# Router logits computed transposed and turned back: weights and moving operand swapped in one product of a fused transformer kernel

## The reference

```python
h = tok_ref(x, ...)                      # 16 images, 196 patches x 768 -> 192, plus class token
h = concatenate([h, txt], axis=1)        # 16 x 325 rows of 192
h = h + attn_ref(layernorm(h), ...)      # q, k, v; scores * decay mask; no softmax
y = layernorm(h)
# the expert layer, all 5200 rows:
logits = y.astype(float32) @ Wg.T        # 128 experts
sig = sigmoid(logits)
choice = sig + e_bias
topk_idx = top_k(choice, 6)              # 6 experts of 128 for every row
topk_w = take(sig, topk_idx); topk_w = 2.5 * topk_w / sum(topk_w)
# every expert takes its first 192 rows: silu(x Wg) * (x Wu) @ Wd, weighted, added back
# plus a shared expert on all rows
h = h + routed + shared
```

## Time and profile before

| | |
|---|---|
| runs | 699.82, 701.12 and 701.9 us, median 701.12 us |
| the profiled execution | 699.24 us, span 697.4 us |
| PE busy | 678.6 us (97%) |
| PEld, DVE, ACT, POOL busy | 635.5, 469.4, 332.0, 201.4 us |
| mean granted TensorE clock | 0.990 of full speed |
| chain that ended last | PE 80%, DVE 10%, issue 4%, ACT 2% |

### The profile page before, as it was taken

The page is one execution under the profiler, slowest core; times in us unless marked ns, Lnnn a source line. Parts: engine busy times, 40 slices in busy tenths (PEclk is TensorE's granted clock), DMA queues, the critical chain, the costliest instruction groups (busy, mean ns, idle before and its releaser), DMA issues.

```text
span 697.4 us, 16667 instructions
## 1 busy us (share of the span) xinstructions
PE 678.6 (97%) x4613; PEld 635.5 (91%) x4614; DVE 469.4 (67%) x1490; ACT 332.0 (48%) x803; POOL 201.4 (29%) x309
## 2 busy tenths in 40 slices
PE   6989999999999999999999999999999999999997
PEld 6879988899988888799999999999999999999997
DVE  2357878888788878765666566666675757576653
ACT  2245555565555666444445343434444434343543
POOL 3022223223223210202323233333333242424240
PEclk9899999999999999999999999999999999999999
DMA  7236434545344321733445454545454545454542
GB/s 232 89 99 210 129 112 148 158 154 152 115 137 141 108 95 63 182 61 63 95 103 108 104 103 106 105 106 104 105 107 102 106 102 107 98 108 97 103 88 56
DMA packets 75188, 79.54 MB, mean 114 GB/s; under 512 B 6505, under 2 KB 67065, under 8 KB 75162
## 3 DMA queue, kind: packets, MB, share of 16 engines
q1 hardware_dynamic: 62538, 65.69, 33.9%
q0 software_dynamic: 11760, 12.31, 11.6%
q10 hardware_dynamic: 864, 1.25, 0.6%
HBM read 51.91 MB, written 19.32 MB: 102 GB/s over the span
## 4 chain that ended last, share of the span: by engine, by line
PE 80%; DVE 10%; issue 4%; ACT 2%; DVEq 1%; POOL 1%; POOLq 0%; ACTq 0%
PE bank L1275 24%; PE bank L1243 12%; PE bank L1292 8%; PE bank L1073 8%; PE bank L1255 8%; PE bank L1061 6%; PE bank L1293 4%; PE bank L1103 3%; PE bank L1217 2%; DVE stats L1454 1%; DVE w_raw L1565 1%; PE bank L1131 1%; PE bank L1088 1%; DVE y_B L1474 1%; DVE h L1490 1%
## 5 line engine op out<-in xcount | busy, mean ns | idle before, releaser
L1740 DVE TENSOR_TENSOR s_inter<-s_gate,bank 128x384 f32<-128x384 f32 (+1 forms) x112 | 60.2, 539 | 73.2 <-PE bank L1275 67.0
L906 ACT ACTIVATE s_gate<-bank 128x384 f32<-128x384 f32 (+1 forms) x112 | 53.5, 478 | 79.1 <-PE bank L1275 79.0
L1292 PE MATMUL bank<-s_dn,s_in_hi 128*128 128x384 f32 (+1 forms) x287 | 88.9, 371 | 0.3 <-DVE s_in_lo L1748 0.2
L727 POOL DMA_INDIRECT result<-y_rows,put_idx x40 | 59.8, 1496 | 57.8 <-DVE y_rows L1727 42.1
L1275 PE MATMUL bank<-all_hiA,s_hi 128*128 (+4 forms) x210 | 73.9, 352 | 0.6 <-DVE s_inter L1740 0.6
L1293 PE MATMUL bank<-s_dn,s_in_lo 128*128 128x192 f32 (+1 forms) x287 | 72.9, 254 | 0.0
L1073 PE MATMUL bank<-w_tok,patches 128*128 128x192 f32 x360 | 68.4, 343 | 4.2 <-DMA patches<-xp 4.0
L798 ACT ACTIVATE y<-h,shift,rstd 128x192 f32<-128x192 f32 (+2 forms) x96 | 45.6, 538 | 54.9 <-POOL shift L658 54.9
L1275 PE MATMUL bank<-all_B,s_lo 128*128 (+4 forms) x210 | 70.2, 334 | 0.0
L1275 PE MATMUL bank<-all_B,s_hi 128*128 (+4 forms) x210 | 70.2, 334 | 0.0
L1275 PE MATMUL bank<-all_loA,s_hi 128*128 (+4 forms) x210 | 70.0, 333 | 0.0
(11 more groups left out here) (216 smaller groups left out, 1831.5 us busy)
## 6 DMA issues: line engine op xcount, KB each, us to landing
raw_gu<-wgu SPq DMA_DIRECT2D x22, 464.0 KB, 5.4
raw_gu<-wgu SPq DMA_DIRECT2D x44, 232.0 KB, 6.0
patches<-xp SPq DMA_DIRECT2D x15, 588.0 KB, 4.3
down_w<-wdn SPq DMA_DIRECT2D x22, 348.0 KB
result<-s_rows POOLq DMA_DIRECT2D x12, 288.0 KB
result<-h SPq DMA_DIRECT2D x16, 192.0 KB
yw_rows<-y SPq DMA_DIRECT2D x16, 192.0 KB
all_hiA<-y_hiA SPq DMA_DIRECT2D x16, 162.5 KB, 2.6
```

The lines of the kernel that those rows point to most:

```text
L727: pool.indirect_dma_start(acc[:, :], bass.IndirectOffsetOnAxis(ap=put_idx[:, h:h + 1], axis=0), y_rows[:, h, :], None, compute_op=ALU.add) ...
L906: act.activation(s_gate[m % 2][0:r, 0:width], up_banks(m, alone)[0][0:r, 0:width], ACT.Silu).then_inc(s_gate_ready, 1)
L1292: pe.matmul(bank[0:r, 0:2 * D], s_in_hi[:, m, rows], s_dn[:, m, :], start=m == 0, stop=False)
L1740: dve.tensor_tensor(s_inter[m % 2][0:r, 0:width], s_gate[m % 2][0:r, 0:width], up, ALU.mult).then_inc(s_inter_ready, 1)
```

## The change

`logits(n)` swaps the two sides: the router matrix is the weights (128 columns) and all S + 1 = 326 columns of the transposed rows move, so five passes do the whole block and the result stands transposed, expert by partition. ACT copies it to SBUF (`lg_evac`, tile `lgT`), in the place where `sigmoid(n)` stood. PE turns it back with three transposes (`turn_logits`) in the next step, behind `turn(n1, n+1)` and ahead of `tokens`, into the same bank. `sigmoid(n)` then runs in ACT's next step, between `turned` and `normed(n2)`. In the tail both are placed by hand between parts of the shared expert.

```diff
--- before.py
+++ after.py
@@ -224,6 +224,7 @@
         cum = sb("cum", [128, 3, SP], BF16)
         patches_1 = sb("patches_1", [128, KC, 256])
         addend_1 = sb("addend_1", [128, D])
+        lgT = sb("lgT", [E, SP])
         zero = left[0:CH, :, :].rearrange("p t n -> p (t n)")[:, 0:YW]
         raw_tables = h1[0:1, :, :].rearrange("p t n -> p (t n)")[:, 0:TABLES]
 
@@ -345,6 +346,8 @@
         pv_mm = sem("pv_mm")
         h1_ready = sem("h1_ready")
         lg_mm = sem("lg_mm")
+        lgT_ready = sem("lgT_ready")
+        lg_turned = sem("lg_turned")
         sig_ready = sem("sig_ready")
         choice_ready = sem("choice_ready")
         best_ready = sem("best_ready")
@@ -806,8 +809,13 @@
                     act.activation(q_B[:, :], qB_ps[0:DB + 1, 0:S], ACT.Identity,
                                    bias=b_q[0:DB + 1, 1:2]).then_inc(qk_ready, 1)
 
+                def lg_evac(n):
+                    act.wait_ge(lg_mm, n + 1)
+                    wait(act, lg_turned, n)
+                    act.activation(lgT[:, 0:S], lg_ps[:, 0:S], ACT.Copy).then_inc(lgT_ready, 1)
+
                 def sigmoid(n):
-                    act.wait_ge(lg_mm, n + 1)
+                    act.wait_ge(lg_turned, n + 1)
                     wait(act, wraw_ready, 3 * n)
                     act.activation(sig[:, 0:2, :], lg_ps[:, 0:2 * E].rearrange("p (t e) -> p t e", t=2), ACT.Sigmoid)
                     act.activation(sig[0:TL[2], 2, :], lg_ps[0:TL[2], 2 * E:3 * E], ACT.Sigmoid).then_inc(sig_ready, 1)
@@ -836,6 +844,7 @@
                     if more:
                         turned(n + 1)
                     if not isinstance(n, int) or n > 0:
+                        sigmoid(n - 1)
                         normed(n2, h1, n)
                     if more:
                         q_evac(n + 1)
@@ -850,7 +859,7 @@
                         normed(n1, h0[:, by_turns(n + 2), :], n + 2)
                     if not isinstance(n, int) or n > 0:
                         weights(n - 1)
-                    sigmoid(n)
+                    lg_evac(n)
 
                 def shared_hi(half, i):
                     act.wait_ge(s_in, 48 + 96 * half)
@@ -940,15 +949,17 @@
                 _, width, tiles = AHEAD[0]
                 last = B - 1
                 turned(last)
+                sigmoid(last - 2)
                 normed(n2, h1, last - 1)
                 q_evac(last)
                 counts(last - 2)
                 split_hi(last - 1)
                 weights(last - 2)
-                sigmoid(last - 1)
+                lg_evac(last - 1)
                 act.wait_ge(h0_ready, B)
                 act.wait_ge(tok_mm, B)
                 s_silu(0, width, 0, PACKED)
+                sigmoid(last - 1)
                 s_silu(0, width, 1, PACKED)
                 normed(n2, h1, last)
                 s_hi_part(0, width, 0)
@@ -960,9 +971,10 @@
                 s_hi_part(0, width, 2)
                 s_silu(0, width, 4, PACKED)
                 act.activation(table_of[:, :], half_neg[0:1, 0:1], ACT.Sigmoid)
-                sigmoid(last)
+                lg_evac(last)
                 s_hi_part(0, width, 3)
                 s_silu(0, width, 5, PACKED)
+                sigmoid(last)
                 s_hi_part(0, width, 4)
                 s_silu(0, width, 6, PACKED)
                 s_hi_part(0, width, 5)
@@ -1133,12 +1145,18 @@
 
                 def logits(n):
                     pe.wait_ge(n2["s_lo"], n + 1)
+                    passes = ((n2["hiA"], g_hi[:, 0, :]), (n2["hiA"], g_lo[:, 0, :]), (n2["loA"], g_hi[:, 0, :]),
+                              (n2["st"], g_hi[:, 1, :]), (n2["st"], g_lo[:, 1, :]))
+                    for i, (x, w) in enumerate(passes):
+                        mm = pe.matmul(lg_ps[:, 0:SP], w, x[:, :], start=i == 0, stop=i == 4)
+                    mm.then_inc(lg_mm, 1)
+
+                def turn_logits(n):
+                    pe.wait_ge(lgT_ready, n + 1)
                     for t in range(3):
                         r, o = TL[t], t * 128
-                        data = (n2["hiA"][:, o:o + r], n2["loA"][:, o:o + r], n2["st"][:, o:o + r])
-                        mm = split_product(lg_ps[0:r, t * E:(t + 1) * E], data, [g_hi[:, h, :] for h in range(2)],
-                                           [g_lo[:, h, :] for h in range(2)])
-                    mm.then_inc(lg_mm, 1)
+                        mm = pe.transpose(lg_ps[0:r, t * E:(t + 1) * E], lgT[:, o:o + r], ident[:, :])
+                    mm.then_inc(lg_turned, 1)
 
                 def running_counts(n):
 
@@ -1154,6 +1172,8 @@
                     if more:
                         turn(n1, n + 1)
                     begun = isinstance(n, int) and n == 0
+                    if not begun:
+                        turn_logits(n - 1)
                     if ahead:
                         tokens(n + 2, 1 if begun else 0)
                     if more:
@@ -1323,6 +1343,7 @@
                 at, width, tiles = AHEAD[0]
                 data = moving(at, width)
                 turn(n1, last)
+                turn_logits(last - 2)
                 pe.wait_ge(h0_ready, B)
                 pe.wait_ge(s_lo_set, 2 * PIECES)
                 pe.wait_ge(big_out, 48 * 4)
@@ -1338,12 +1359,15 @@
                     if m == 3:
                         pe.wait_ge(h1_ready, B)
                     s_up(0, data, width, m, PACKED, PACKED_FREE[m])
+                    if m == 1:
+                        turn_logits(last - 1)
                 turn(n2, last, last - 1)
                 running_counts(last - 1)
                 s_up(0, data, width, 5, PACKED, PACKED_FREE[5])
                 logits(last)
                 pe.wait_ge(ct_ready, last)
                 s_up(0, data, width, 6, PACKED, PACKED_FREE[6])
+                turn_logits(last)
                 s_up(0, data, width, 7, PACKED, PACKED_FREE[7])
                 data_1 = moving(*AHEAD[1][0:2])
                 s_up(1, data_1, AHEAD[1][1], 0, ALONE, 3)
```

## The result

The change makes the kernel slower: 716.33 us (median of 4, 714.88 to 717.19) against 700.47 us for the kernel before on the same chip (median of 4, 698.3 to 701.9). The ratio is 1.0221 with a 95% interval of 1.0198 to 1.0244, so 15.9 us are lost (13.9 to 17.1 by the interval). The forecast was a loss of 16.8 us and a time of 717.9 us, with a range of 712 to 724. The profiled execution took 717.19 us, with a span of 715.3 us; it is the longest of the four.

What follows compares the result with a forecast made beforehand. A ring through `tokens`, DVE, POOL and ACT's `y` was taken to bound the loop, not PE's work. Loop 10.6, tail 5.2 and clock 1.0 sum to 16.8 us over 701.12, giving 717.9 us, range 712 to 724.

Steps and rivals of the forecast that it cites:

- The ring: Loop: `tokens`, DVE, POOL, ACT's `y`, transposes of n1, `tokens` again set the step; a late ACT result costs in full.
- The signs named ahead: Loop: no idle before `lgT`, transposes 0.05 to 0.13 us behind `y`, `logits` some 0.85, `turn_logits` waiting some 0.6.
- the second way round: Loop: PE's own queue (`score`, `attend`, `logits`) takes about as long as the ring, balanced to some 0.2 us.
- The term for the loop: Late `lgT` puts `tokens` 0.88 us later in each of twelve steps, 10.6 us in all.
- The tail: After the loop: four more table loads make `choices(15)` 5.2 us late, with no slack left to absorb it.
- The rival that the tail hides its loads: Tail: other parts of the shared expert cover the loads; 711.7 us, chance 12% for hidden in part or wholly.
- The loads' own price: Tail: each table load takes 1.28 us and the next instruction starts at its end, without a further drain.
- The rival that rested on it: Tail: each switch costs the load and about as much again; tail 10.7 us, time 723.4 us, chance 3%.
- The clock: Tail: PE idle some 3.5 us before the late `s_in_lo` brings one fall of the granted clock, 1.0 us.
- The clock in the loop: Rival: PE's longer waits in each step bring four to eight clock falls, 722 to 726 us, chance 14%.
- The saved PE work: Counted as nothing in the loop; rival that it counts: 16 x 0.31 = 5.0 us less, 696.1 us; faster 2%.
- the condition under which it would count: Loop: `w_rows` standing behind `lgT` on ACT, and `y` ending before the shorter `logits`.

Runs made afterwards that it cites:

- E1: Changed kernel with ACT's copy of the logits (`lg_evac`) ahead of the weighted rows in the loop; 708.38 us, ratio 1.0133 to the kernel before.
- E7: Kernel before, with PE's `value` behind the second half of `tokens` and DVE's `token_rows` ahead of `values`; 696.11 us, ratio 0.9923.
- E2: Changed kernel with the product and `sigmoid` of before for images 14 and 15, so five table loads; 707.58 us, ratio 1.0134 to the kernel before.
- E3: Changed kernel with the tail's `sigmoid` right behind `lg_evac` and `turn_logits(last - 1)` right behind its logits, so five table loads; 707.89 us, ratio 1.0137.
- E4: Kernel before with three of the five passes in each tile of the logits, low part of the router matrix left out; 698.4 us, ratio 0.9982.
- E8: E7's move plus the new product in the loop, the copy ahead of `w_rows` and the old tail; 693.35 us, ratio 0.9892 to the kernel before.
- E6: Changed kernel with `turn_logits` moved behind the first half of `tokens` on PE; 711.96 us, ratio 1.0155 to the kernel before.

## Why the prediction was right, step by step

**The ring** held. The signs named ahead are there: `lgT` starts without idle time, the transposes of n1 stand 0.13 us behind `y`, `logits` take 0.85 us (0.70 from the first to the fifth start, and 0.15). One sign came out smaller: `turn_logits` waits 0.35 us for `lgT` by the profile, where 0.6 was named. E1 proves the place: with the copy ahead of `w_rows`, and nothing else, three quarters of the loss per step go (0.74 to 0.18 us).

One part of the picture was wrong without harm to the sum. The prediction called the second way round "PE's own queue" and balanced with the ring to 0.2 us. The balance was right, but that way leads over DVE's `y_B`, for which PE waited 0.40 us. PE's own queue is shorter by more: E7's step of 14.14 us still holds a wait of 0.32 us.

**The term for the loop was too large**, 0.88 us a step and 10.6 us in all; measured were 0.74 and 9.1 ((236.94 - 67.81) / 11 = 15.38 us between starts of `tokens`, where 15.5 was forecast). At the place itself the price was right: `tokens` starts 0.90 us later behind `y`. But from the first half of `tokens` to the second it takes 4.98 us instead of 5.11. Before, a pass of `query` had waited for DVE's `y_B`; `turned` did not move, so DVE is ready earlier relative to PE, and that small wait went. I had taken it that nothing on the ring gives time back. Of the 9.1 us the twelve steps are 8.9; the other 0.2 come in the step before the tail, for which nothing was forecast. That a `sigmoid` one step later costs nothing in the loop held: DVE was idle 1.15 us before `h` at 182.72, against 1.05 in the earlier trace rows.

**The tail** was forecast at 5.2 us and measured at 5.5. `y` of image 15 starts at 269.40, later than in the earlier trace rows by 10.94 us, of which 9.1 are the loop's: 1.83 us where 1.85 was worked out. Of the 0.3 us that came on top about 0.1 is due to the clock: it had fallen behind an earlier wait (last section), and `logits(15)` ends at 275.35, when ACT had been free for `lgT` since 275.25. E2 and E3 confirm the cause. The rival that the tail hides its loads is refuted; DVE idled 3.47 us.

**The loads' own price.** A load took 1.28 us, and its neighbours touch it on both sides (276.12 + 1.28 = 277.40, the next at 277.41). By the Trainium skill, "ScalarE: Activation LUTs", section "What ACT_TABLE_LOAD costs", a drain of 1380 ns would come on top; the trace agrees on the load (1283 ns is the mean of its nine loads) and shows no such drain. The rival that rested on it falls.

**The clock** was, in proportion, the term most in error: one fall, 1.0 us forecast, 2.2 us measured. The wait was of the forecast length (3.11 us, some 3.5 expected), but the fall covered a stretch in which PE, and with it the path to `order`, was matmuls alone. Ten passes of 384 columns take 3.3 us (284.65 to 287.98) instead of 1.8, and the `s_dn` passes behind them 1.5 instead of 0.8. The earlier row that the price was taken from the earlier trace rows had only 2.16 us of matmuls in it.

**The clock in the loop** didn't fall, with 0.93 us of PE waits in each step: that rival is refuted. **The saved PE work** was worth nothing in the changed kernel, as said. E4 shows the same from the other side, with 0.8 us for 9.4 us of work. The forecast named the condition under which it would count, the copy ahead of `w_rows` and a `y` that ends before `logits`; E8 has both (`y` ends at 162.79, `logits` at 163.26), and there the new product doesn't cost; but of the 0.31 us of PE work only 0.07 us a step come back.

The sum, 9.1 + 5.5 + 2.2, comes to the forecast 16.8 because two errors cancel (-1.5 in the loop, +0.3 and +1.2 in the tail). That the total agrees to a tenth is luck; the terms agree to 0.3 to 1.5 us. And the medians, which were what was forecast, are 15.9 us apart.

## What to carry to other kernels

When an engine is busy for nearly all of a loop, follow one step backwards from a single instruction until the way closes on itself. Work that is saved beside such a ring is worth nothing (E4), one small result that another engine delivers late moves the whole ring (a 0.42 us copy and the transposes behind it put `tokens` 0.9 us later behind `y`, and the step grew by 0.74), and the new product in the loop turns from a loss to none that shows once the ring is shortened and the copy stands first (E7, E8). A result that the bottleneck engine needs belongs at the head of its producer's queue: moving one call ahead of another was worth 6.7 us here (15.9 against 9.2). In a hand-woven tail, put functions of different activation tables together before anything else, and price a long wait of PE (2.4 and 3.1 us here) at the wait plus the matmuls that follow it at half the clock.

## What was not expected of the hardware

The half clock after the 3.11 us wait cost 2.2 us on top of the wait. The clock was down while PE still stood idle (0.67 from 282 to 284 us, where matmuls begin at 283.25). A wait of 2.43 us earlier in the same tail (PE idle before the transposes of image 15's n2 at 270.87) was also followed by a granted clock of 0.61 and 0.54 (272 to 276 us), this time when PE was already at work again, with passes of 326 columns 0.27 us apart instead of 0.15. In the changed kernel ACT was late itself and lost 0.1 us by it; in E1 and E6, where the same happened, ACT's `lgT` waited 0.41 and 0.32 us for these passes. E2 and E3, without the long waits, have a mean granted clock of 0.992, while the changed kernel, E1 and E6, with them, have 0.983 to 0.986.
